# Order of turns, spreads and C copies in the scan steps of a twelve-layer decoder kernel

## The chip, the core and the metric

One Trainium2 chip, one of its cores. The metric is the device time of one launch in microseconds (us). The kernel before took 2616.81, 2618.38 and 2629.36 us in three runs, median 2618.38 us. The profile shown here is of one further execution, which took 2617.74 us.

## The reference

Twelve layers, four decoder blocks of attention, cross block and feed-forward, each followed by a layer norm over 4 sequences of 256 tokens, width 256. The change touches only the cross block of the first two decoder blocks (layers 1 and 4), a selective state-space scan: 256 inner channels, 16 states.

```python
x = einsum('ed,bld->bel', in_proj_w, ctx); u = silu(causal_conv4(x) + conv_b)
x_dbl = einsum('ke,bel->bkl', x_proj_w, u)          # 8 rows dt, 16 rows B, 16 rows C
delta = softplus(dt_proj_w @ dt_lo + dt_proj_b); A = -exp(A_log)
def step(state, t):                                  # for each token t
    state = state * exp(delta_t * A) + (delta_t * u_t) * B_t
    y_t = sum_n state[n] * C_t[n]
y = (y + D * u) * silu(z)                            # z: the layer's own input
```

## The kernel before, in words

The program has a queue of instructions for each engine, written out in layer order; semaphores join them, and every engine executes its queue strictly in order. TensorE (PE), VectorE (DVE), ScalarE (ACT), GpSimd (POOL) and the DMA queue of SyncE (SP) take part. SP issues only the loads of weights for these layers.

The class `StateSpace` makes the scan over time one DVE instruction for each state and half of the tokens. So a layer has 32 steps (`STEPS`): steps 0 to 15 are the 16 states for tokens 0 to 511, steps 16 to 31 the same for tokens 512 to 1023. Channels lie on partitions, in two groups (`CH`), so a step works on 128 x 1024 values. One step k is:

- *spread* (`tensor_spread`, L824, PE): two matmuls with a picking matrix write row B of state k to all partitions of PSUM bank 4, and row C to bank 5. There is one bank for each, so spread k waits until ACT has copied C of step k-1 (`s_c_read`) and until DVE has read B of step k-1 (`s_driven`).
- *drive* (`vector_drive`, L925, DVE): `du` times bank 4, into one of two PSUM buffers (banks 0 and 1, or 2 and 3).
- *exponentials* (L1003, ACT, two instructions) make the decay of step k, in one of two buffers, so they wait for scan k-2.
- *C copy* (L1008, ACT): bank 5 to SBUF, into one of two buffers `c`, so it waits for the product of step k-2 (`s_outed`).
- *scan* (L936, DVE): decay and drive into the state, one of two buffers.
- *product* (L1054, POOL): state times C, into `out`, one of two buffers, so it waits for the turns of step k-2 (`s_added`).
- *turns* (`tensor_add`, L842, PE): eight transposing matmuls add `out` to the sums in PSUM banks 6 and 7. After step 15 and after step 31 eight more add the skip term, and ACT reads the sums out (*y read*, L1016, `scalar_y`). The turns of step 16 wait for the first y read, since they start the sums anew.

The order is set by slots. `vector_slot(s)` puts drive s+1 ahead of scan s. `scalar_slot(s)` puts the work of step s+1 on ACT. `tensor_slot(s)` puts spread s+1 and then the turns of step s-1 on PE. `gpsimd_slot(s)` is product s. Layer norm and the next layer follow, and they need the last y read.

A class `SmallHeads` can host such a scan beside its own work (`hosts`), but `build` makes both scan layers unhosted, so its line in the diff adds nothing to this program.

Of the kernel before, what the change touches and what calls it, by code (L numbers as in the profile page):

```python
# [22 lines left out]
ALU = mybir.AluOpType  # L23
ACT = mybir.ActivationFunctionType
# [8 lines left out]
CH = D // P  # L33
# [4 lines left out]
BANK = 512  # L38
# [32 lines left out]
class Arena:  # L71


    def __init__(self, tensor, words):
        self.tensor, self.words, self.at = tensor, words, 0
# [24 lines left out]
def bcast(ap, axis, n):  # L100

    shape = list(ap.shape)
    return ap.unsqueeze(axis).broadcast_to(shape[:axis] + [n] + shape[axis:])
# [76 lines left out]
class LayerNorm:  # L180
# [43 lines left out]
    def tensor(self, pe):  # L224
        e, nc, l = self.e, self.e.nc, self.l
        for pair in range(TILES // 2):
            pe.wait_ge(e.x_ready, TILES * l + 2 * pair + 2)
            for half in range(2):
                for c in range(CH):
                    last = nc.tensor.transpose(e.bank[self.turn_bank(pair)][:, c * D + half * P:c * D + half * P + P],  # L230
                                               e.x_tok[:, 2 * pair + half, c * P:(c + 1) * P], e.ident[:])
            last.then_inc(e.xt_psum, 1)
# [14 lines left out]
class SmallHeads:  # L247
# [137 lines left out]
    def tensor(self, pe):  # L385
# [121 lines left out]
            if t % 2:  # L507
                last.then_inc(e.y_ready, 1)
        if self.hosts:
            self.beside.tensor_slot(pe, STEPS)  # L510

    def proj_bank(self, blk, s, half):
        return (0 if blk or self.hosts else 4) + 2 * s + half
# [183 lines left out]
STEPS = HALVES * STATES  # L697
# [6 lines left out]
class StateSpace:  # L704
# [10 lines left out]
    def __init__(self, e, l, arena, name, room=None):  # L715
        self.e, self.l, self.name = e, l, name
        self.hosted = room is not None
        a, big = arena, e.big
# [12 lines left out]
        splitting = a.take(2 * TOKENS)  # L731
        self.rest = splitting[:, 0:TOKENS]
        self.mid = splitting[:, TOKENS:TOKENS + BANK].bitcast(BF16)
        self.low = splitting[:, TOKENS + BANK:2 * TOKENS].bitcast(BF16)
        self.c = splitting[:, 0:2 * BANK].rearrange("p (k t) -> p k t", k=2)
        if not self.hosted:
            big.reset()
        self.u = big.take(CH, TOKENS)
# [12 lines left out]
        s = e.sem  # L751
# [97 lines left out]
    def tensor_slot(self, pe, s):  # L849
        if s + 1 < STEPS:  # L850
            self.tensor_spread(pe, s + 1)
        if s:
            self.tensor_add(pe, s - 1)

    def tensor(self, pe):
        if not self.hosted:
            self.wait_start(pe)
            self.tensor_in(pe)
            self.tensor_low(pe)
            self.tensor_dt(pe)  # L860
            self.tensor_spread(pe, 0)
            for s in range(STEPS + 1):
                self.tensor_slot(pe, s)

    def vector_conv(self, dve):
# [126 lines left out]

    def scalar_step(self, act, k):
        a, n = self.e.nc.scalar.activation, k % STATES
        if k == 0:
            act.wait_ge(self.s_cleared, 1)
            act.wait_ge(self.s_delta, 1)
            self.e.act_chain.join(act)
        else:
            act.wait_ge(self.s_scanned, k - 1)  # L1000
        for j in range(CH):
            seqs = lambda ap: ap.rearrange("p (b t) -> p b t", b=2)[:, :, 1:]
            last = a(seqs(self.decay[:, k % 2, j, :]), seqs(self.delta[:, j, self.cols(k)]), ACT.Exp, scale=self.a_neg[:, j, n:n + 1])  # L1003
        last.then_inc(self.s_decay, 1)
        act.wait_ge(self.s_bc_psum, k + 1)
        if k >= 2:
            act.wait_ge(self.s_outed, k - 1)
        a(self.c[:, k % 2, :], self.e.bank[5][:], ACT.Copy).then_inc(self.s_c_read, 1)  # L1008

    def scalar_y(self, act, half):  # L1010
        a = self.e.nc.scalar.activation
# [37 lines left out]
    def gpsimd_slot(self, pool, s):  # L1049
        pool.wait_ge(self.s_c_read, s + 1)  # L1050
        pool.wait_ge(self.s_scanned, s + 1)
        if s >= 2:
            pool.wait_ge(self.s_added, s - 1)
        self.e.nc.gpsimd.tensor_tensor(self.out[:, s % 2], self.state[:, s % 2], bcast(self.c[:, s % 2, :], 1, CH), ALU.mult).then_inc(self.s_outed, 1)  # L1054

    def gpsimd(self, pool):
        if not self.hosted:
# [1359 lines left out]
```

## Time and profile before

| what | value |
|---|---|
| median of three runs | 2618.38 us |
| the profiled execution, its span | 2617.74 us, 2616.0 us |
| PE, its weight loads | 1932.2 us (74%), 1283.9 us (49%) |
| DVE | 1528.2 us (58%) |
| ACT | 832.8 us (32%) |
| POOL | 557.0 us (21%) |
| chain that ended last, share of the span | PE 55%, DVE 30%, ACT 5%, issue 5%, POOL 3% |

The shares are averages over twelve layers with different limits. The scans run from 198.50 to 330.28 us and from 562.81 to 696.15 us of the span; the rest of the program is not touched. In the timeline a row is one instruction, or some of one line in a row (x8). In brackets stands how long the engine was idle before it, and which instruction released it. Rows of PE are matmuls, rows of PEld the weight loads beside them.

### The profile page before, as it was taken

The numbers are of one execution on the slowest core, as the hardware profiler recorded it, in microseconds if no ns is written. First come the engines' busy times: TensorE is split into PE (matmuls) and PEld (weight loads), VectorE is DVE, ScalarE is ACT, GpSimd is POOL, SyncE is SP. The second block draws the span as 40 slices with busy tenths as digits, with TensorE's granted clock in tenths as the row PEclk, the third lists the DMA queues.
The fourth block names the chain that finished last, engine by engine and source line by source line (L and its number), as shares of the span: only waits on it lengthen the run. The fifth ranks groups of instructions, "written<-read, shape, count | busy, mean of one in ns | idle before, by whom it ended". The sixth has DMA issues, their size and how long they took to land.

```text
span 2616.0 us, 28127 instructions
## 1 busy us (share of the span) xinstructions
PE 1932.2 (74%) x9950; PEld 1283.9 (49%) x9950; DVE 1528.2 (58%) x2480; ACT 832.8 (32%) x2085; POOL 557.0 (21%) x353
## 2 busy tenths in 40 slices
PE   5646678646546766888889846445999999999886
PEld 3523444324323455666667524324666765555743
DVE  4368757677795814555553299997466324445114
ACT  1344402254322053555552111111455214444000
POOL 1304410014302042333331055564000000000010
PEclk9975577655567988888889877776999999999966
DMA  3000020100000110000010100000001000000000
GB/s 104 7 33 1 0 55 5 50 1 0 8 33 15 22 42 9 13 11 12 12 56 1 73 0 0 0 0 0 8 10 50 1 15 9 12 12 19 6 27 16
DMA packets 25737, 49.11 MB, mean 19 GB/s; under 512 B 6262, under 2 KB 19603, under 8 KB 24092
## 3 DMA queue, kind: packets, MB, share of 16 engines
q1 hardware_dynamic: 25644, 47.85, 6.1%
q8 instruction: 60, 0.98, 0.2%
q14 instruction: 33, 0.27, 0.0%
HBM read 42.20 MB, written 1.05 MB: 17 GB/s over the span
## 4 chain that ended last, share of the span: by engine, by line
PE 55%; DVE 30%; ACT 5%; issue 5%; POOL 3%; SPq 1%; DMA 1%; DVEq 0%; ACTq 0%; POOLq 0%
PE banks L1309 7%; PE banks L1278 7%; PE banks L1318 7%; PE banks L1247 6%; DVE big L1989 5%; PE banks L1301 4%; DVE big L1985 3%; PE banks L842 3%; DVE big L556 2%; PE banks L1543 2%; DVE big L936 2%; POOL big L1054 2%; PE banks L463 2%; PE banks L474 2%; DVE arena L1365 1%
## 5 line engine op out<-in xcount | busy, mean ns | idle before, releaser
L1384 DVE COPY arena<-banks 128x512 f32<-128x512 f32 x196 | 135.6, 692 | 329.8 <-PE banks L1301 326.6
L222 POOL TENSOR_TENSOR ln_rstd<-ln_var_eps,neg_half 128x2 f32<-128x2 f32 x48 | 37.4, 780 | 1057.8 <-DVE ln_var_eps L210 1057.8
L1278 PE MATMUL banks<-big 128*128 128x256 f32 x784 | 235.6, 413 | 6.0 <-ACT big L1420 4.4
L1309 PE MATMUL banks<-arena,big 128*128 128x256 f32 x784 | 227.5, 414 | 6.3 <-DVE arena L1384 6.3
L1441 ACT ACTIVATE arena<-banks,arena 128x256 f32<-128x256 f32 x392 | 193.4, 500 | 62.2 <-DVE arena L1358 43.1
L842 PE MATMUL banks<-ident,big 128*128 128x128 f32 x544 | 130.4, 419 | 94.0 <-POOL big L1054 90.0
L1459 ACT ACTIVATE big<-banks 128x256 f32 (+1 forms) x196 | 75.3, 384 | 348.1 <-PE banks L1309 348.1
L842 PEld LDWEIGHTS banks<-ident,big 128*128 128x128 f32 x544 | 105.3, 219 | 149.5 <-POOL big L1054 135.3
L1318 PE MATMUL banks<-arena,big 128*128 128x256 f32 x784 | 176.8, 385 | 1.9 <-ACT big L1459 1.9
L1247 PE MATMUL banks<-x_feat,arena 128*128 128x512 f32 x392 | 177.5, 596 | 0.0
L1309 PEld LDWEIGHTS banks<-arena,big 128*128 128x128 f32 x784 | 140.7, 197 | 64.4 <-DVE arena L1384 43.0
L1365 DVE TENSOR_SCALAR arena<-arena 128x256 f32<-128x256 f32 x392 | 166.1, 466 | 6.9
L1352 DVE TENSOR_REDUCE arena<-banks 128x2 f32<-128x512 f32 x196 | 134.2, 685 | 60.5 <-PE banks L1278 42.5
L1318 PEld LDWEIGHTS banks<-arena,big 128*128 128x128 f32 x784 | 148.5, 191 | 29.1 <-issue 6.2
L1054 POOL TENSOR_TENSOR big<-big,arena 128x1024 f32<-128x1024 f32 x64 | 128.4, 2007 | 149.8 <-DVE big L936 104.4
L1278 PEld LDWEIGHTS banks<-big 128*128 128x128 f32 x784 | 136.5, 201 | 33.7 <-ACT big L1420 8.8
L1949 PE MATMUL banks<-ident,big 128*128 128x128 f32 x128 | 29.9, 425 | 162.7 <-POOL big L2038 162.7
L936 DVE TENSOR_TENSOR_SCAN big<-big,banks 128x1024 f32<-128x1024 f32 x64 | 145.7, 2279 | 0.0
L1989 DVE SCALAR_TENSOR_TENSOR big<-big,arena 128x2048 f32<-128x2048 f32 x32 | 141.2, 4411 | 1.1
L1301 PE MATMUL banks<-ident,arena 128*128 128x128 f32 x784 | 128.1, 289 | 18.4 <-DVE arena L1365 18.4
L203 DVE TENSOR_TENSOR x_tok<-x_tok,banks 128x512 f32<-128x512 f32 x40 | 27.4, 685 | 184.2 <-PE banks L1318 100.1
L1301 PEld LDWEIGHTS banks<-ident,arena 128*128 128x128 f32 x784 | 99.4, 148 | 65.6 <-DVE arena L1365 33.0
(311 smaller groups left out, 3514.6 us busy)
## 6 DMA issues: line engine op xcount, KB each, us to landing
big<-big SPq DMA_DIRECT2D x32, 64.0 KB, 2.3
arena<-in_L0f_w SPq DMA_DIRECT2D x1, 2048.0 KB, 8.0
arena<-in_L1a_wo SPq DMA_DIRECT2D x1, 2048.0 KB
arena<-in_L1f_gv SPq DMA_DIRECT2D x1, 2048.0 KB
arena<-in_L2a_qk_w SPq DMA_DIRECT2D x1, 2048.0 KB
big<-big SPq DMA_DIRECT2D x64, 32.0 KB
arena<-in_L2x_wo SPq DMA_DIRECT2D x1, 2048.0 KB
arena<-in_L2x_q_w SPq DMA_DIRECT2D x16, 128.0 KB, 2.0
```

What stands on the lines that cost most here:

```text
L842: ins = e.nc.tensor.matmul(e.bank[6 + t // 2][:, at:at + P], src[:, j, t * P:(t + 1) * P], e.ident[:], is_transpose=True, start=(first and ...
L936: self.e.nc.vector.tensor_tensor_scan(flat(self.state[:, s % 2]), flat(self.decay[:, s % 2]), flat(self.drive[s % 2]), 0.0, ALU.mult, ALU. ...
L1054: self.e.nc.gpsimd.tensor_tensor(self.out[:, s % 2], self.state[:, s % 2], bcast(self.c[:, s % 2, :], 1, CH), ALU.mult).then_inc(self.s_ou ...
L1247: last = mm(B[half][:], self.q_w[:, head_par, c, :], e.x_feat[:, c, cols], start=(c == 0), stop=(c == CH - 1))
L1278: last = mm(ps[:, h * SEQ:(h + 1) * SEQ], q[:, b * SEQ + h * P:b * SEQ + (h + 1) * P], k[:, b * SEQ:(b + 1) * SEQ], start=True, stop=not s ...
L1301: last = nc.tensor.transpose(B[4 + u % 2][:, kc * SEQ + h * P:kc * SEQ + (h + 1) * P], self.probs[:, u % 2, h, kc * P:(kc + 1) * P], e.ide ...
L1309: last = mm(slot, self.v[:, 2 * b + kc, :], self.probs_t[:, u % 2, kc, :], start=(kc == 0), stop=(kc == 1))
L1318: last = mm(e.y_bank(t), self.out[:, h, t * P:(t + 1) * P], wo[h], start=(h == 0), stop=(h == self.heads - 1 and not self.bias))
L1365: last = v.tensor_scalar(self.probs[:, u % 2, h, :], self.probs[:, u % 2, h, :], self.inv[:, u % 2, h:h + 1], None, ALU.mult)
L1384: v.tensor_copy(self.probs_t[:, u % 2].rearrange("p a b -> p (a b)"), B[4 + u % 2][:]).then_inc(self.turn_read, 1)
L1441: last = a(self.probs[:, u % 2, h, :], B[2 + u % 2][:, h * SEQ:(h + 1) * SEQ], ACT.Exp, bias=self.neg_max[:, u % 2, h:h + 1], scale=scale, ...
L1989: v.scalar_tensor_tensor(self.chosen[h], self.sums, self.final[:, h, 7:8], self.sums, ALU.is_ge, ALU.mult, accum_out=self.kept[:, h:h + 1] ...
```

## The change

Three things are moved or made larger; no instruction is added or removed.

- `tensor_slot(s)` puts the turns of step s-2, not s-1, behind spread s+1, and so there is one more slot at the end. The matching line in `SmallHeads` is not used here.
- `c` has four buffers of 512 values in place of two, in the room that the splitting of B and C into bf16 parts used before the steps. The copy of step k waits for product k-4, not k-2.
- In `scalar_step` the C copy, with its waits, stands ahead of the two exponentials of the same step. For step 0 it stands ahead of the waits for the cleared decay buffer and for delta, too.

```diff
--- before.py
+++ after.py
@@ -507,7 +507,7 @@
             if t % 2:
                 last.then_inc(e.y_ready, 1)
         if self.hosts:
-            self.beside.tensor_slot(pe, STEPS)
+            self.beside.tensor_slot(pe, STEPS), self.beside.tensor_slot(pe, STEPS + 1)
 
     def proj_bank(self, blk, s, half):
         return (0 if blk or self.hosts else 4) + 2 * s + half
@@ -732,7 +732,7 @@
         self.rest = splitting[:, 0:TOKENS]
         self.mid = splitting[:, TOKENS:TOKENS + BANK].bitcast(BF16)
         self.low = splitting[:, TOKENS + BANK:2 * TOKENS].bitcast(BF16)
-        self.c = splitting[:, 0:2 * BANK].rearrange("p (k t) -> p k t", k=2)
+        self.c = splitting.rearrange("p (k t) -> p k t", k=4)
         if not self.hosted:
             big.reset()
         self.u = big.take(CH, TOKENS)
@@ -849,8 +849,8 @@
     def tensor_slot(self, pe, s):
         if s + 1 < STEPS:
             self.tensor_spread(pe, s + 1)
-        if s:
-            self.tensor_add(pe, s - 1)
+        if s >= 2:
+            self.tensor_add(pe, s - 2)
 
     def tensor(self, pe):
         if not self.hosted:
@@ -859,7 +859,7 @@
             self.tensor_low(pe)
             self.tensor_dt(pe)
             self.tensor_spread(pe, 0)
-            for s in range(STEPS + 1):
+            for s in range(STEPS + 2):
                 self.tensor_slot(pe, s)
 
     def vector_conv(self, dve):
@@ -992,6 +992,10 @@
 
     def scalar_step(self, act, k):
         a, n = self.e.nc.scalar.activation, k % STATES
+        act.wait_ge(self.s_bc_psum, k + 1)
+        if k >= 4:
+            act.wait_ge(self.s_outed, k - 3)
+        a(self.c[:, k % 4, :], self.e.bank[5][:], ACT.Copy).then_inc(self.s_c_read, 1)
         if k == 0:
             act.wait_ge(self.s_cleared, 1)
             act.wait_ge(self.s_delta, 1)
@@ -1002,10 +1006,6 @@
             seqs = lambda ap: ap.rearrange("p (b t) -> p b t", b=2)[:, :, 1:]
             last = a(seqs(self.decay[:, k % 2, j, :]), seqs(self.delta[:, j, self.cols(k)]), ACT.Exp, scale=self.a_neg[:, j, n:n + 1])
         last.then_inc(self.s_decay, 1)
-        act.wait_ge(self.s_bc_psum, k + 1)
-        if k >= 2:
-            act.wait_ge(self.s_outed, k - 1)
-        a(self.c[:, k % 2, :], self.e.bank[5][:], ACT.Copy).then_inc(self.s_c_read, 1)
 
     def scalar_y(self, act, half):
         a = self.e.nc.scalar.activation
@@ -1051,7 +1051,7 @@
         pool.wait_ge(self.s_scanned, s + 1)
         if s >= 2:
             pool.wait_ge(self.s_added, s - 1)
-        self.e.nc.gpsimd.tensor_tensor(self.out[:, s % 2], self.state[:, s % 2], bcast(self.c[:, s % 2, :], 1, CH), ALU.mult).then_inc(self.s_outed, 1)
+        self.e.nc.gpsimd.tensor_tensor(self.out[:, s % 2], self.state[:, s % 2], bcast(self.c[:, s % 4, :], 1, CH), ALU.mult).then_inc(self.s_outed, 1)
 
     def gpsimd(self, pool):
         if not self.hosted:
```

PE's queue, at the start of a scan layer and in the middle and at the end of it (L824 the spreads, two matmuls for each step; L842 the turns, eight for each step; L230 the transposes of the layer norm that follows):

```order
 L803 MATMUL banks<-big,arena 104x512 x4
 L814 MATMUL banks<-arena 128x512 x4
-L824 MATMUL banks<-arena 128x512 x6
+L824 MATMUL banks<-arena 128x512 x8
 L842 MATMUL banks<-ident,big 128x128 x8
 L824 MATMUL banks<-arena 128x512 x2
```

Four spreads, not three, stand ahead of the first turns. From there on spreads and turns take turns as before, each group of turns one spread later.

```order
 L842 MATMUL banks<-ident,big 128x128 x8
 L824 MATMUL banks<-arena 128x512 x2
-L842 MATMUL banks<-ident,big 128x128 x8
-L824 MATMUL banks<-arena 128x512 x2
-L842 MATMUL banks<-ident,big 128x128 x32
+L842 MATMUL banks<-ident,big 128x128 x40
 L230 MATMUL banks<-ident,x_tok 128x128 x16
```

At the layer's end five groups of eight turns, not four, stand behind the last spread.

ACT's queue at the first steps (before, L1003 are the exponentials and L1008 the C copy; in the changed kernel the copy is L998 and the exponentials are L1007; L991 ends the softplus, L1023 scales `u` for the skip term):

```order
 L985 ACTIVATE big<-big 128x512 x4
 L991 ACTIVATE big<-big,arena 128x2048 x4
-L1003 ACTIVATE big<-big,arena 128x2x255 x2
-L1008 ACTIVATE arena<-banks 128x512
-L1003 ACTIVATE big<-big,arena 128x2x255 x2
-L1008 ACTIVATE arena<-banks 128x512
+L998 ACTIVATE arena<-banks 128x512
+L1007 ACTIVATE big<-big,arena 128x2x255 x2
+L998 ACTIVATE arena<-banks 128x512
+L1007 ACTIVATE big<-big,arena 128x2x255 x2
 L1023 ACTIVATE big<-big,arena 128x512 x4
```

Copy and exponentials of each step have changed places. The queues of DVE, POOL and SP are the same in both kernels.

## Rows read from the trace of the kernel before

**Rows 1.** Groups by line: name, shapes, count; busy us, mean ns; idle before.
```profile
L936 DVE TENSOR_TENSOR_SCAN big<-big,banks 128x1024 f32<-128x1024 f32 x64 | 145.7, 2279 | 0.0
...
L1054 POOL TENSOR_TENSOR big<-big,arena 128x1024 f32<-128x1024 f32 x64 | 128.4, 2007 | 149.8 <-DVE big L936 104.4 <-ACT arena L1008 42.0 <-issue 3.4
...
L1003 ACT ACTIVATE big<-big,arena 128x510 f32<-128x510 f32 x128 | 85.2, 712 | 99.9 <-DVE big L936 84.6 <-POOL big L1047 15.3
...
L925 DVE TENSOR_TENSOR banks<-big,banks 128x1024 f32<-128x1024 f32 x64 | 78.7, 1229 | 55.1 <-PE banks L824 52.2
...
L1008 ACT ACTIVATE arena<-banks 128x512 f32<-128x512 f32 x64 | 38.2, 597 | 51.8 <-POOL big L1054 51.8
```

**Rows 2.** Timeline, steady steps, first scan layer: start, length (us), engine, line, operation [idle].
```profile
232.43 2.28 DVE L936 TENSOR_TENSOR_SCAN big<-big,banks 128x1024 f32<-128x1024 f32 x1
...
234.81 1.23 DVE L925 TENSOR_TENSOR banks<-big,banks 128x1024 f32<-128x1024 f32 x1
234.84 2.00 POOL L1054 TENSOR_TENSOR big<-big,arena 128x1024 f32<-128x1024 f32 x1 [2.94 <-DVE big L936]
235.95 2.28 DVE L936 TENSOR_TENSOR_SCAN big<-big,banks 128x1024 f32<-128x1024 f32 x1
...
236.89 1.97 PE L842 MATMUL banks<-ident,big 128*128 128x128 f32 x8 [2.12 <-POOL big L1054]
236.93 0.60 ACT L1008 ACTIVATE arena<-banks 128x512 f32<-128x512 f32 x1 [0.86 <-POOL big L1054]
...
238.36 2.00 POOL L1054 TENSOR_TENSOR big<-big,arena 128x1024 f32<-128x1024 f32 x1 [1.53 <-ACT arena L1008]
...
238.65 1.06 PE L824 MATMUL banks<-arena 96*128 96x512 bf16 x2
239.75 1.23 DVE L925 TENSOR_TENSOR banks<-big,banks 128x1024 f32<-128x1024 f32 x1 [1.52 <-PE banks L824]
...
240.89 2.28 DVE L936 TENSOR_TENSOR_SCAN big<-big,banks 128x1024 f32<-128x1024 f32 x1
```

**Rows 3.** Timeline, first steps of the first and of the second scan layer.
```profile
194.26 1.23 DVE L925 TENSOR_TENSOR banks<-big,banks 128x1024 f32<-128x1024 f32 x1
...
196.29 1.04 PE L824 MATMUL banks<-arena 96*128 96x512 bf16 x2 [21.25 <-ACT arena L1008]
...
197.37 1.23 DVE L925 TENSOR_TENSOR banks<-big,banks 128x1024 f32<-128x1024 f32 x1 [1.88 <-PE banks L824]
...
198.50 2.28 DVE L936 TENSOR_TENSOR_SCAN big<-big,banks 128x1024 f32<-128x1024 f32 x1
...
562.81 2.28 DVE L936 TENSOR_TENSOR_SCAN big<-big,banks 128x1024 f32<-128x1024 f32 x1
```

**Rows 4.** Timeline, turn from first to second half, first scan layer.
```profile
265.80 3.67 PE L842 MATMUL banks<-ident,big 128*128 128x128 f32 x16 [0.71 <-POOL big L1054]
...
269.27 1.06 PE L824 MATMUL banks<-arena 96*128 96x512 bf16 x2
...
271.26 1.02 ACT L1016 ACTIVATE big<-banks 128x1024 f32<-128x1024 f32 x1
```

**Rows 5.** Timeline, end of the first and of the second scan layer.
```profile
325.82 4.46 DVE L936 TENSOR_TENSOR_SCAN big<-big,banks 128x1024 f32<-128x1024 f32 x2
...
330.19 3.07 DVE L954 TENSOR_TENSOR big<-big,x_feat 128x512 f32<-128x512 f32 x2
...
330.41 2.30 POOL L1054 TENSOR_TENSOR big<-big,arena 128x1024 f32<-128x1024 f32 x1 [0.18 <-DVE big L936]
...
336.98 1.29 DVE L954 TENSOR_TENSOR big<-big,x_feat 128x512 f32<-128x512 f32 x2 [3.71 <-ACT big L1016]
...
691.69 4.46 DVE L936 TENSOR_TENSOR_SCAN big<-big,banks 128x1024 f32<-128x1024 f32 x2
```

**Rows 6.** Windows of L842 alone: stretch, its us, busy (count), clock, DMA.
```profile
236.50:239.00 2.50, 1.97 (x8) 1.57 (x8) 0.50 0.00 0
272.20:273.50 1.30, 1.10 (x8) 0.86 (x8) 1.00 0.00 0
```

## The prediction

> **What bounds the kernel now.** I read the page first, and its 74% for PE says little, because the change touches only the two scan layers. So I read the groups by line for the lines of a scan step, then the timeline of some steps in the middle, and then the two ends of the stage, where a rule for the middle may fail.
>
> In the groups by line [rows 1] the reader should see that DVE does one drive (1.229 us) and one scan (2.279 us) for each step, 3.51 us, and that no other engine has so much: ACT two exponentials and a copy (2 x 0.712 + 0.597 = 2.02 us), POOL one product (2.007 us). Yet DVE idles 55.1 us ahead of its drives, 52.2 of it released by the spreads on PE. That idle time is what can be had here.
>
> The timeline [rows 2] shows its shape. From 234.81 on DVE does drive and scan without a gap: scan 232.43 to scan 235.95 is 3.52 us, the period of a step without a wait. The next drive waits 1.52 us. From scan 232.43 to scan 240.89, two steps, are 8.46 us, or 4.23 for a step. I follow the ring of waits through these rows: the scan ends at 234.71, its product on POOL runs from 234.84 to 236.84, its turns on PE start at 236.89, the spread queued behind them starts at 238.65 and ends at 239.71, the drive starts at 239.75 and the scan at 240.89. Each row starts 0.04 to 0.13 us after the end of the one before, or overlaps it on one engine; nothing in the ring is free. It takes 8.46 us and comes back to DVE two steps on. So a scan step is bound by a ring of DVE, POOL and PE, and its weak place is that a spread, which needs nothing from the product, stands behind turns that do.
>
> **The moved turns.** No instruction is added. With the turns of step s-2 behind spread s+1, the same ring (scan, product, turns, next spread, drive, scan) comes back three steps on: 8.46 / 3 = 2.82 us a step. That is under DVE's 3.52, so the wait goes and DVE is next. I check the other candidates for a period.
>
> PE's own turn: turns and spread back to back run from 236.89 to 239.71 [rows 2], 2.82 us. In the new rhythm I put the end of a drive at 0. The spread runs from 0.13 to 1.19. The product of two steps ago ends 0.90 after this point: its scan ended as this drive started, at -1.23, plus 0.13 and 2.00. So the turns start behind the spread at about 1.2 and end at 3.2, before the next drive ends at 3.52. There are 0.3 us to spare, the smallest margin of this argument.
>
> Buffers: a product takes 2.00 and its turns 1.97 us, which with two `out` buffers is about 2 us a step, and product s waits for turns s-2, ended some 2.7 us before it (3.2 against 5.9). The state buffer returns after product and scan, 4.4 us in two steps. No new wait decides there.
>
> **The four buffers for C and the order on ACT.** With the turns moved alone the next ring would be: scan, product (ends 236.84), C copy of two steps on (236.93 to 237.53 in [rows 2]), spread, drive, scan. With 0.13 for the handoff to PE the spread would run from 237.66 to 238.72, the drive start at 238.76 and the scan at 239.90: 7.47 us in two steps, 3.74 a step. That is 0.22 over DVE's, so both parts are needed for the whole gain. With four buffers the copy waits for a product four steps back, which has long ended. The copy ahead of the exponentials then runs as soon as its spread ends, at 1.2 to 1.9 in my rhythm, in a gap where ACT otherwise waits for the scan that ends at 2.28; the exponentials run from 2.35 to 3.7 and are needed at 7.0. So head-of-line waiting on ACT is covered by 3.3 us. I price it at nothing; were the cover gone, the exponentials would be late by the copy's 0.60 us.
>
> **The start.** Before, drive 0 starts at 194.26 and ends at 195.49, but spread 1 starts only at 196.29, after the copy behind the first exponentials, and drive 1 follows at 197.37 [rows 3]. The first copy is now done before drive 0. Spread 1 starts at 195.62, 0.67 earlier, and so do drive 1 and the first scan. The second layer has the same queues, so 0.67 there too.
>
> **The turn between the halves.** The sixteen turns of step 15 take 3.67 us, the next spread starts 3.47 after their start, and the y read takes 1.02 [rows 4]. I count from the end of scan 15. The product ends at 2.13, spread 18 at about 2.5. The sixteen turns run from 2.5 to 6.2, spread 19 from 6.0 to 7.0. Drive 19 is due at 7.1 (two periods and 0.1). It just fits. The y read runs from about 6.3 to 7.3, the turns of step 16 from 7.35 to 9.3, spread 20 ends at 10.2, drive 20 is due at 10.6. So nothing is added here; if one of these is late by some tenths, each layer loses as much once, under 1 us.
>
> **The end.** The last two scans stand together (4.46 us for both in [rows 5]), and then product 31 and its turns follow as before. The turns of step 30 must still precede those of step 31, and they end before product 31 does in both orders. Nothing won or lost. TensorE has granted clock 0.50, the 1.2 GHz level, for most of this stage, and eight turns take 1.97 us; in a short stretch at 1.00, the 2.4 GHz level, they took 1.10 [rows 6]. If the denser PE gets the higher level, only the 24 turns at the end are on the path, and the products stand between them: at most about 1 us a layer. I count 0 and keep it for the lower end.
>
> **The sum.** First layer: scan 0 starts at 198.50 - 0.67 = 197.83. Thirty periods of 3.52 are 105.6, so scan 30 starts at 303.43 and scan 31 ends at 307.89, against 325.82 + 4.46 = 330.28 before [rows 3, 5]: 22.4 us. Second layer: 562.81 - 0.67 + 105.6 + 4.46 = 672.20, against 696.15: 23.9 us. Together 46.3. As a check, 15 waits of 1.52 less a normal gap of 0.1 are 21 us a layer. The profiled execution took 2617.74 us, so 2571.4; its time is 0.64 below the median, which gives 2572. Everything behind the layers waits for the y read and moves with it. Each 0.1 us by which the period misses 3.52 costs 6.0 us.
>
> **Rivals.**
>
> *PE becomes the bound.* Its two waits in a step now fall apart, the spread behind the drive and the turns behind the spread, so the pipeline may not stay filled. Unoverlapped, a turn of PE is 0.13 + 1.06 + 0.05 + 1.97 = 3.21 us; with a weight load of 0.20 (1.57 / 8 [rows 6]) exposed at each wait 3.61, and with another 0.13 as handoff 3.74. That is 0.09 to 0.22 over DVE, or 5 to 13 us: 2577 to 2585. Against it: in rows 2 the spread starts behind the turns with no such gap. DVE would then still show short waits for L824.
>
> *DVE and POOL share something and slow each other, and it ends slower.* This has its place at the drives, which now always start as a product starts. The row for it is at the layer's end: the two products L954 on DVE, beside a product on POOL, take 3.07 us, and two without it 1.29; the one on POOL takes 2.30, not 2.00 [rows 5]. If each step paid the same 1.78 us, the period would be 5.30 and the kernel would take 2572 + 60 x 1.78 = 2679. From a stretch of 0.77 us a step (46.3 / 60) it is slower than before. Against it: the product at 234.84 covers the whole drive at 234.81 and the start of the scan at 235.95, and both keep their usual 1.23 and 2.28 [rows 2]; half of the steps before were already like this, and the mean of all 64 drives is 1229 ns [rows 1].
> The Trainium skill ("SBUF — State Buffer", section "Who interferes with whom") says that a DVE instruction with two inputs in SBUF contends with a GpSimd instruction that reads SBUF, and one with a single input there, outside certain fast modes, does not. L954 reads `big` and `x_feat`, the drive `big` and PSUM `banks`: by that rule, and the trace agrees, the price is 0 and the time stays 2572.
>
> *The wait only moves.* If the ring were bound on POOL's wait for the copies (1.53 us ahead of the product at 238.36 [rows 2]) or on ACT behind spreads, DVE would wait ahead of its scans instead and the period stay 4.23: 2618. Against it: the ring above closes without that copy, to 0.01 us.
>
> **How the numbers follow.** The forecast has a chance of 0.83, with an own range of 2565 to 2578: 1 us a layer for each end effect, and a period of up to 3.6. PE as the bound 0.11, the wait only moved 0.03, DVE and POOL in each other's way 0.03. The range 2562 to 2588 takes in the higher clock below and PE as the bound above, and leaves out the last two. A measurement of this kernel can tell about 0.5%, 13 us, from no change, so below 2605 is faster: 0.83 + 0.11 = 0.94. Same 0.03, slower 0.03.
>
> **What would show it.** In the profile after: scans every 3.52 us; the idle time ahead of L925 down from 55.1 to under 5 us, nearly all at the starts; drive, scan and product with their old means of 1229, 2279 and 2007 ns; ACT's idle time ahead of the C copy put down to the spreads, no longer to POOL; the last scans ending near 308 and 650 us (672 less the first layer's 22). The prediction is wrong if DVE still waits for L824 in the middle of the layers (PE bound), if its drives grow longer, or if it begins to wait ahead of L936.

## The result, and the profile after

The changed kernel took 2577.66 us (median of 4 runs, 2571.83 to 2591.45), the kernel before 2617.82 (4 runs, 2616.81 to 2629.36). The ratio is 0.984, 95% interval 0.981 to 0.987: faster by 1.6%. The profiled execution took 2571.83 us, its span 2570.1, against 2617.74 and 2616.0 before. Run again beside the experiments it had ratios of 0.9815 (0.978 to 0.985) and 0.9817 (0.977 to 0.986).

The groups by line of the changed kernel (the copy is now L998, the exponentials L1007) answer to [rows 1]:

```profile
L936 DVE TENSOR_TENSOR_SCAN big<-big,banks 128x1024 f32<-128x1024 f32 x64 | 145.7, 2279 | 0.0
...
L1054 POOL TENSOR_TENSOR big<-big,arena 128x1024 f32<-128x1024 f32 x64 | 128.4, 2007 | 103.6 <-DVE big L936 100.5 <-ACT arena L998 3.1
...
L1007 ACT ACTIVATE big<-big,arena 128x510 f32<-128x510 f32 x128 | 85.1, 712 | 40.1 <-DVE big L936 25.7 <-POOL big L1047 14.4
...
L925 DVE TENSOR_TENSOR banks<-big,banks 128x1024 f32<-128x1024 f32 x64 | 78.7, 1229 | 8.9 <-PE banks L824 2.4
...
L998 ACT ACTIVATE arena<-banks 128x512 f32<-128x512 f32 x64 | 38.3, 598 | 62.5 <-PE banks L824 62.5
```

The mean durations of scan, product, exponentials, drive and copy are the old ones to within 1 ns, and DVE has no idle time ahead of its scans. What fell is idle time: 55.1 to 8.9 us ahead of the drives, of which the spreads on PE release 2.4, and no longer 52.2. ACT's copies now wait for spreads and no longer for products.

The timeline of a step in the middle, which answers to [rows 2]:

```profile
226.01 1.23 DVE L925 TENSOR_TENSOR banks<-big,banks 128x1024 f32<-128x1024 f32 x1
226.04 2.00 POOL L1054 TENSOR_TENSOR big<-big,arena 128x1024 f32<-128x1024 f32 x1 [1.53 <-DVE big L936]
227.15 2.28 DVE L936 TENSOR_TENSOR_SCAN big<-big,banks 128x1024 f32<-128x1024 f32 x1
...
227.39 1.01 PE L824 MATMUL banks<-arena 96*128 96x512 bf16 x2 [0.81 <-DVE banks L925]
...
228.19 1.91 PE L842 MATMUL banks<-ident,big 128*128 128x128 f32 x8
228.44 0.60 ACT L998 ACTIVATE arena<-banks 128x512 f32<-128x512 f32 x1 [1.17 <-PE banks L824]
229.46 1.33 ACT L1007 ACTIVATE big<-big,arena 128x510 f32<-128x510 f32 x2 [0.43 <-DVE big L936]
229.53 1.23 DVE L925 TENSOR_TENSOR banks<-big,banks 128x1024 f32<-128x1024 f32 x1
...
230.91 1.01 PE L824 MATMUL banks<-arena 96*128 96x512 bf16 x2 [0.80 <-DVE banks L925]
```

DVE goes from drive to scan to drive: 226.01 to 229.53 is 3.52 us, each step. The spread starts 0.15 us after the drive's end, and behind it stand turns of a product that had ended at 228.04, so PE is never kept from a spread. It idles 0.81 us ahead of each, waiting for the drive. The start answers to [rows 3]:

```profile
202.45 1.23 DVE L925 TENSOR_TENSOR banks<-big,banks 128x1024 f32<-128x1024 f32 x1
...
203.83 1.01 PE L824 MATMUL banks<-arena 96*128 96x512 bf16 x2 [20.61 <-DVE banks L925]
204.88 1.23 DVE L925 TENSOR_TENSOR banks<-big,banks 128x1024 f32<-128x1024 f32 x1 [1.20 <-PE banks L824]
...
206.01 2.28 DVE L936 TENSOR_TENSOR_SCAN big<-big,banks 128x1024 f32<-128x1024 f32 x1
```

Drive 1 starts 2.43 us after drive 0 (3.11 before), scan 0 3.56 after it (4.24 before). At the turn between the halves, which answers to [rows 4], spread 19 starts 3.42 us after the sixteen turns and ends at 267.90, and drive 19 starts on time at 268.29:

```profile
263.42 3.62 PE L842 MATMUL banks<-ident,big 128*128 128x128 f32 x16
...
266.84 1.06 PE L824 MATMUL banks<-arena 96*128 96x512 bf16 x2
268.29 1.23 DVE L925 TENSOR_TENSOR banks<-big,banks 128x1024 f32<-128x1024 f32 x1
```

The ends of the two layers answer to [rows 5]:

```profile
311.70 4.46 DVE L936 TENSOR_TENSOR_SCAN big<-big,banks 128x1024 f32<-128x1024 f32 x2
...
316.07 3.07 DVE L954 TENSOR_TENSOR big<-big,x_feat 128x512 f32<-128x512 f32 x2
...
316.29 2.31 POOL L1054 TENSOR_TENSOR big<-big,arena 128x1024 f32<-128x1024 f32 x1 [0.18 <-DVE big L936]
...
318.65 3.67 PE L842 MATMUL banks<-ident,big 128*128 128x128 f32 x16 [0.52 <-POOL big L1054]
...
649.12 4.46 DVE L936 TENSOR_TENSOR_SCAN big<-big,banks 128x1024 f32<-128x1024 f32 x2
...
656.07 2.58 PE L842 MATMUL banks<-ident,big 128*128 128x128 f32 x16 [0.52 <-POOL big L1054]
```

From the start of scan 0 to the end of scan 31 it is 110.15 us (206.01 to 316.16) and 110.14 us (543.44 to 653.58), in place of 131.78 and 133.34. That is 21.6 and 23.2 us less. The rest of the program is where I had not looked. This table has the time in us from the start of one layer norm's last write of `x_feat` to that of the next, as the rows of L238 in the traces give it; layers 5 to 10 are together:

| layers | before | after | difference | after, third profile | before, again |
|---|---|---|---|---|---|
| 0 | 145.86 | 154.04 | +8.18 | 143.66 | 154.30 |
| 1 (scans) | 204.02 | 182.29 | -21.73 | 181.51 | 204.22 |
| 2 | 85.74 | 84.68 | -1.06 | 85.65 | 85.85 |
| 3 | 74.54 | 69.06 | -5.48 | 74.51 | 74.45 |
| 4 (scans) | 205.27 | 182.59 | -22.68 | 181.35 | 205.38 |
| 5 to 10 | 1766.67 | 1766.47 | -0.20 | 1770.10 | 1770.21 |
| 11 | 132.83 | 129.86 | -2.97 | 132.76 | 129.87 |

The two scan layers give 44.4 of the 45.9 us; layers that were not touched gave 9.7 and took 8.2. The last two columns, of experiments below, show that most of this comes and goes in both kernels. Layer 3's short time does not stand in them; two other kernels below (B in SBUF, and each third drive on POOL) have the same 69.06.

Within layer 4 something went the other way. Its first scan starts 52.8 us after the last write of layer 3's norm has ended, 52.1 before, where 51.4 was to be had; in the two other profiles of the changed kernel it is 51.4. So the first profile has a loss of 1.4 us there, all of it ahead of drive 0.

### The profile page after: what moved, and what is told of

Its sections match the earlier page's. It is cut to its first block, busy times and chain, and to the rows that moved or that the text cites. A ratio compares the mean times of both kernels' runs of the same rounds, so it can differ in the third digit from the quotient of the medians.

```text
span 2570.1 us, 28114 instructions
## 1 busy us (share of the span) xinstructions
PE 1921.5 (75%) x9941; PEld 1275.6 (50%) x9950; DVE 1528.0 (59%) x2480; ACT 832.6 (32%) x2085; POOL 557.0 (22%) x353
## 3 DMA queue, kind: packets, MB, share of 16 engines
HBM read 42.20 MB, written 1.05 MB: 17 GB/s over the span
## 4 chain that ended last, share of the span: by engine, by line
PE 53%; DVE 34%; issue 5%; ACT 4%; SPq 1%; POOL 1%; DMA 1%; DVEq 0%; ACTq 0%; POOLq 0%
PE banks L1309 7%; PE banks L1278 7%; PE banks L1318 7%; PE banks L1247 6%; DVE big L936 6%; DVE big L1989 6%; PE banks L1301 4%; DVE big L1985 3%; DVE big L556 3%; PE banks L1543 2%; PE banks L463 2%; PE banks L474 2%; DVE arena L1365 1%; DVE big L1637 1%; DVE arena L1994 1%
## 5 line engine op out<-in xcount | busy, mean ns | idle before, releaser
L1949 PE MATMUL banks<-ident,big 128*128 128x128 f32 x128 | 30.0, 425 | 162.1 <-POOL big L2038 162.1
L824 PE MATMUL banks<-arena 96*128 96x512 bf16 x128 | 63.2, 595 | 96.7 <-DVE banks L925 95.5
L842 PE MATMUL banks<-ident,big 128*128 128x128 f32 x544 | 124.0, 406 | 7.9 <-POOL big L1054 6.9
```

## The experiments

Scans 0 to 31 of each scan layer, in us, with the time of each kernel. In the two kernels profiled more than once the scans repeat within 0.1 us a layer, while the span varies by up to 9.4. The ratio is to runs of before on the same chip; their median was 2629.10 beside the fourth, 2620.91 beside the others:

| kernel | period | first layer | second | median us | ratio to before |
|---|---|---|---|---|---|
| before | 3.53 and 4.94 by turns | 131.78 | 133.34 | 2620.91 | 1 |
| moved turns alone | 3.52 and 3.85 by turns | 115.06 | 115.36 | 2593.60 | 0.9905 (0.988-0.993) |
| copy ahead, four buffers, alone | 3.52 and 4.94 by turns | 133.45 | 133.54 | 2628.34 | 1.0022 (1.0005-1.0038) |
| moved turns, copy ahead, two buffers | 3.52 and 3.85 by turns | 116.06 | 115.78 | 2600.57 | 0.9894 (0.984-0.994) |
| moved turns, four buffers | 3.52 | 110.09 | 110.19 | 2579.37 | 0.9828 (0.979-0.986) |
| the full change, again | 3.52 | 110.09 | 110.11 | 2575.56 | 0.9815 (0.978-0.985) |

**Moved turns alone.** The turns move as in the change, with one slot more at the end; the excerpt has the turns.

```diff
-        if s:
-            self.tensor_add(pe, s - 1)
+        if s >= 2:
+            self.tensor_add(pe, s - 2)
```

> Only the turns move behind the next spread; C keeps two buffers and its place behind the exponentials. My theory (rings of waits): the ring through the C copy (scan 2.28, product 2.00, copy 0.60, spread 1.06, drive 1.14, handoffs) takes 7.47 us in two steps, so the period of a step falls from 4.23 to 3.74 us, scans 0 to 31 take 30 x 3.74 + 4.46 = 116.7 us in each layer (131.8 and 133.3 before), and the kernel about 32 us less than before, near 2586; ahead of its drives DVE still waits some 0.2 us a step, released by spreads that wait for the C copy. Rival 1 (the moved turns are all that matters): period 3.52, 110.1 us a layer, about 45 us less. Rival 2 (the wait was the copy's, not the turns'): period 4.23, no gain.

Measured 115.06 and 115.36 us a layer, 34.7 us less in the scans than before, and 27 us less in the time of the kernel (2593.60 against 2620.91), which misses the expected 2586. In its profile layer 6, which nothing here touches, took 231.0 us, and 218.8 to 221.7 in the profiles of before and of the full change; why is not known. Two other kernels below had 231.0 there too. Timeline of this kernel, where L1008 is the C copy and L1003 the exponentials:

```profile
220.86 2.00 POOL L1054 TENSOR_TENSOR big<-big,arena 128x1024 f32<-128x1024 f32 x1 [1.84 <-DVE big L936]
...
222.95 0.60 ACT L1008 ACTIVATE arena<-banks 128x512 f32<-128x512 f32 x1 [0.86 <-POOL big L1054]
...
223.61 1.03 PE L824 MATMUL banks<-arena 96*128 96x512 bf16 x2 [1.10 <-ACT arena L1008]
...
224.68 1.23 DVE L925 TENSOR_TENSOR banks<-big,banks 128x1024 f32<-128x1024 f32 x1 [0.42 <-PE banks L824]
225.82 2.28 DVE L936 TENSOR_TENSOR_SCAN big<-big,banks 128x1024 f32<-128x1024 f32 x1
```

The ring is the one expected: product, copy, spread, drive. It closes in 7.37 us for two steps, not 7.47, since the spread follows the copy by 0.06 us, not 0.13. So the moved turns alone bring three quarters of the gain in the scans (34.7 of 44.8 us), and then the C copy binds.

**Copy ahead and four buffers, turns unmoved.** An excerpt; `c` has four buffers, and the copy's old place behind the exponentials is gone, as in the change.

```diff
+        act.wait_ge(self.s_bc_psum, k + 1)
+        if k >= 4:
+            act.wait_ge(self.s_outed, k - 3)
+        a(self.c[:, k % 4, :], self.e.bank[5][:], ACT.Copy).then_inc(self.s_c_read, 1)
         if k == 0:
```

> Only ACT's side of the change: four buffers for C and the copy ahead of the exponentials; the turns stay where they were. My theory: the ring through product, turns and the spread behind them is untouched, period 4.23 us, scans 0 to 31 131 to 133 us a layer; the earlier first copy saves 0.67 us a layer, so about 1 us less than before, not to be told from no change. ACT's waits for the product go, POOL's waits for the copies too, and nothing comes of it. Rival 2 (the wait was the copy's): period 3.5 to 3.7, 30 to 45 us less.

Measured 133.45 and 133.54 us a layer and 2628.34 us, 0.2% over before. Groups by line of this kernel:

```profile
L925 DVE TENSOR_TENSOR banks<-big,banks 128x1024 f32<-128x1024 f32 x64 | 78.7, 1229 | 55.6 <-PE banks L824 52.5
...
L998 ACT ACTIVATE arena<-banks 128x512 f32<-128x512 f32 x64 | 38.2, 597 | 143.6 <-PE banks L824 143.6
```

DVE's wait for spreads is 52.5 us, as before, though the copy no longer waits for products at all. So the rival that the copy held DVE falls. That its first layer takes 1.7 us more than before is not the rhythm; at the turn of the halves two steps take 4.75 and 5.64 us (5.23 and 3.55 before). I did not expect it. The rows put most of it down to the clock: the turns of step 16 and the spread behind them took 1.97 and 1.06 us, where before they had met the higher level and took 1.10 and 0.61. The y read, which now stood right behind the exponentials, came 0.35 us later after the start of the sixteen turns.

**Moved turns and four buffers, copy left behind the exponentials.** The turns move as in the change; the excerpt has the copy.

```diff
-        if k >= 2:
-            act.wait_ge(self.s_outed, k - 1)
-        a(self.c[:, k % 2, :], self.e.bank[5][:], ACT.Copy).then_inc(self.s_c_read, 1)
+        if k >= 4:
+            act.wait_ge(self.s_outed, k - 3)
+        a(self.c[:, k % 4, :], self.e.bank[5][:], ACT.Copy).then_inc(self.s_c_read, 1)
```

> The moved turns and four buffers for C, with the copy left behind the exponentials. My theory: the copy of step k starts 1.33 us after scan k-2 ends, ends at about 2.05, its spread at 3.2, and the next drive is due at 3.6, so the period is 3.52 us all the same, 110.1 us a layer; only the first step loses its 0.67 us a layer. About 44 us less than before, within 2 us of the full change. Rival (the order on ACT is needed): the spread is late behind the copy, DVE waits 0.1 to 0.3 us a step, period 3.6 to 3.8, 6 to 17 us slower than the full change.

110.09 and 110.19 us a layer: the whole rhythm. Its groups by line:

```profile
L925 DVE TENSOR_TENSOR banks<-big,banks 128x1024 f32<-128x1024 f32 x64 | 78.7, 1229 | 10.3 <-PE banks L824 3.9
...
L824 PE MATMUL banks<-arena 96*128 96x512 bf16 x128 | 63.8, 600 | 100.1 <-ACT arena L1008 96.2 <-DVE banks L925 2.8 <-DVE arena L898 1.1
```

PE's idle time is now put down to the copy (96.2 us), not to the drive, so the copy does come later; but DVE waits for spreads only 3.9 us in all, 1.5 more than with the full change. From drive 0 to scan 0 it is 4.24 us again, and 3.56 with the full change. So the order on ACT is worth its 0.67 us at the start of a layer, and beyond it at most 0.1 us a layer.

**Moved turns, copy ahead, two buffers.** The C copy stands ahead as in the full change, with `k % 2` and the wait for `s_outed` at k - 1.

> Moved turns, and the copy ahead of the exponentials, but with the old two buffers for C. My theory: the copy still waits for the product two steps back, so the ring through the copy decides as with the turns alone (3.52 and 3.85 us by turns there, scans 115.1 to 115.4 us a layer); the order on ACT changes nothing but the start, so 115 us a layer again. Rival (head-of-line blocking on ACT): the copy at the head now keeps the exponentials back until the product is done, the decay becomes late, DVE waits ahead of its scans and the period exceeds 3.69 us by some tenths, up to 0.60, the copy's length: 118 to 133 us a layer.

116.06 and 115.78 us, 1.0 and 0.4 more than with the turns alone. Its groups by line:

```profile
L936 DVE TENSOR_TENSOR_SCAN big<-big,banks 128x1024 f32<-128x1024 f32 x64 | 145.9, 2279 | 0.9 <-ACT big L1007 0.9
...
L925 DVE TENSOR_TENSOR banks<-big,banks 128x1024 f32<-128x1024 f32 x64 | 78.7, 1229 | 19.4 <-PE banks L824 15.9
```

Head-of-line blocking (an instruction that waits at the head of a queue keeps back those behind it) is there, but small: DVE waits 0.9 us in all ahead of scans for late exponentials, 0.60 of it ahead of the last scan of the first layer. The rival's 0.60 us a step came in that one step and not in the rhythm.

**More work on PE.** The first matmul of each spread done twice (`(0, 0, 1)`), and both done twice (shown, the second line cut off at its end):

```diff
-        for n in range(2):
+        for n in (0, 0, 1, 1):
             last = self.e.nc.tensor.matmul(self.e.bank[4 + n][:], ...
```

> The full change, with the first matmul of each spread done twice (same result): 0.53 us more for PE in each step. PE idles 0.81 us ahead of each spread in the profile of the full change. My theory: it still fits, period 3.52, scans 110.1 to 110.3 us a layer, PE's idle time per step down to about 0.3. Rival (PE nearly the bound, as in my forecast's first rival): the 0.3 us of margin that I gave are overdrawn by 0.2, period 3.7, 116 us a layer.

> The full change, with both matmuls of each spread done twice: 1.06 us more for PE in each step, more than the 0.81 us that it idles. My theory: now PE binds. Counting from the end of a spread: drive starts at 0.04 and ends at 1.27; the turns begin 0.2 us before 0, and the next spread 1.76 after their start, at 1.56, ending at 3.63; the next drive 3.67. Period 3.67, scans near 114.6 us a layer, about 9 us more than the full change, with DVE idle 0.15 us ahead of each drive. Rival (waits between PE's groups empty its pipeline, 0.2 us each): period 3.9 or more, 121 us a layer. Rival (PE doesn't matter at all): 110.1.

Both took 110.1 us a layer (110.08 and 110.08, 110.09 and 110.08), and 2580.46 and 2583.86 us. The first came as expected. The second broke my expectation: at the 1.2 GHz level its 1.06 us of added work are more than the 0.81 us that PE had idle, and there was no loss. Windows 220 to 240 us, of the kernels with one and with two more, and of the full change; the clock is the number behind the last "(x...)":

```profile
220.00:240.00 20.00, 12.64 (x64) 8.01 (x65) 19.48 (x12) 11.10 (x18) 11.63 (x6) 0.83 0.01 1
```

```profile
220.00:240.00 20.00, 10.53 (x66) 6.92 (x67) 19.48 (x12) 10.90 (x17) 11.98 (x6) 1.00 0.01 2
```

```profile
220.00:240.00 20.00, 15.64 (x58) 10.23 (x59) 19.48 (x12) 10.48 (x17) 10.98 (x6) 0.50 0.00 1
```

With more work PE was granted the 2.4 GHz level, for part of this window and for all of it, where the full change stayed at the 1.2 GHz level. Over the scans of each layer the mean granted clock was 0.87 and 0.95, against 0.53. So PE's longer turn took less time.

In some steps the kernel with one more matmul stood at the 1.2 GHz level, and there it shows PE's margin:

```profile
231.55 1.44 PE L824 MATMUL banks<-arena 96*128 96x512 bf16 x3 [0.84 <-DVE banks L925]
232.79 1.91 PE L842 MATMUL banks<-ident,big 128*128 128x128 f32 x8
235.07 0.94 PE L824 MATMUL banks<-arena 96*128 96x512 bf16 x3 [0.38 <-DVE banks L925]
```

The three matmuls take 1.44 us in place of 1.01, the turns the usual 1.91, and 0.38 us of idle time are left of 0.81, in the same period of 3.52. The timeline of the kernel with both matmuls twice:

```profile
224.88 1.02 PE L824 MATMUL banks<-arena 96*128 96x512 bf16 x4 [1.62 <-DVE banks L925]
...
225.74 1.04 PE L842 MATMUL banks<-ident,big 128*128 128x128 f32 x8
...
227.03 1.23 DVE L925 TENSOR_TENSOR banks<-big,banks 128x1024 f32<-128x1024 f32 x1
```

Four matmuls take 1.02 us, where two took 1.01, and the turns 1.04 in place of 1.91; from the spread's start to the end of the turns it is 1.90 us in place of 2.71. So this kernel did not try PE's margin at the 1.2 GHz level; the rows above did. It shows instead that the stage has none of its time from PE: with the turns at nearly half their length, DVE's rhythm is 3.52 all the same.

**B read from SBUF by the drive.** ACT copies both banks at once (an excerpt, with `...` where a line is shortened):

```diff
-        a(self.c[:, k % 4, :], self.e.bank[5][:], ACT.Copy).then_inc(self.s_c_read, 1)
+        a(self.bc[:, k % 4], self.e.banks[:, 4:6, :], ACT.Copy).then_inc(self.s_c_read, 1)
-        ... self.drive[k % 2], self.du[:, :, self.cols(k)], bcast(self.e.bank[4][:], 1, CH), ALU.mult)
+        ... self.drive[k % 2], self.du[:, :, self.cols(k)], bcast(self.bc[:, k % 4, 0, :], 1, CH), ALU.mult)
```

> The full change, but ACT copies the spread of B with that of C (1024 in place of 512 values, 1.02 us by the y read of the same size), and the drive on DVE reads B from SBUF, so it has two inputs there and runs beside the product on POOL. It measures the disputed cost of DVE and POOL in each other's way. By the rule (two SBUF inputs contend, one doesn't) and the start of the drive 0.03 us ahead of the product: the product waits for the drive, its row grows from 2.00 to about 3.2 us, and the period stays at 3.52 to 3.6. If the product gets in first, the drive grows from 1.23 to up to 3.2 us and the period to 5.5 (170 us a layer). If nothing contends: both keep 1.23 and 2.00 and the period is 3.52. In no case does that say that the changed kernel pays anything: its drive has one SBUF input.

2592.41 us, 114.02 and 114.03 us a layer, at a period of 3.52 to 3.53 but for two steps of 5.42, where the copy stood on ACT behind the skip scaling or the y read and the drive was 1.0 and 1.8 us late for that reason. The timeline shows both orders of arrival:

```profile
209.72 2.00 POOL L1054 TENSOR_TENSOR big<-big,arena 128x1024 f32<-128x1024 f32 x1 [6.92 <-DVE big L936]
...
210.73 2.08 DVE L925 TENSOR_TENSOR banks<-big,arena 128x1024 f32<-128x1024 f32 x1 [1.15 <-ACT arena L998]
...
225.68 1.23 DVE L925 TENSOR_TENSOR banks<-big,arena 128x1024 f32<-128x1024 f32 x1
225.71 3.05 POOL L1054 TENSOR_TENSOR big<-big,arena 128x1024 f32<-128x1024 f32 x1 [0.47 <-ACT arena L998]
```

Where the product was first (209.72), the drive took 2.08 us, ending 1.09 us after the product. Where the drive was first by 0.03 us (225.68), it kept its 1.23 and the product took 3.05 us, 1.05 more; that is so in most steps (55 of the 64 products took 3.04 to 3.06 us; their mean is 2.93). By the section of the Trainium skill named in the prediction ("SBUF — State Buffer", "Who interferes with whom") a VectorE instruction with two inputs in SBUF contends with a GpSimd instruction that reads SBUF, and the issue order decides who blocks. The trace agrees: the later one was slowed, and by nearly the time that it stood beside the other (0.85 of 0.99 us, 1.05 of 1.20). In the changed kernel, whose drive has one input in PSUM, the products have their 2.007 us.

**The full change, and the kernel before, profiled again.**

> The full change unaltered, on the same chip as the three parts. Scans 0 to 31 take 110.1 us in each layer, 21.7 and 23.2 us less than before. The time in between: in its first profile layer 0, which is not touched, took 8.2 us longer than in the profile of before, at a lower granted clock between 80 and 120 us of the span. My theory: this is how the clock happens to rise in that layer, and has nothing to do with the change, so it comes and goes between executions of one kernel; the time is then 2570 to 2592 us and the spans of the two scan stages do not vary. Rival: the change itself costs time in layer 0 or in other layers, and the same 8 us stand there each time.

> The full change once more, for the two kernels beside it. Scans 0 to 31 110.1 us a layer, 2567 to 2592 us. It also gives one more execution of layer 0, which no kernel here touches: it ended at 145.9 us of the span in the profile of before and at 154.0, 151.0 in the two of the full change, 154 in two kernels with moved turns and 143.7 in others. My theory: two or three outcomes of when the clock rises, met by any of the kernels. Rival: the full change fixes the late one.

> The kernel before, unaltered, profiled again: is its layer 0 always the fast one? My theory: it can end near 146 or near 154 us, with the time 8 us apart, and scans 0 to 31 take 131.8 and 133.3 us within 2. Rival: always near 146.

The stages of the scans repeat to 0.1 us: 110.09 and 110.11, 110.13 and 110.11, and for before 131.76 and 133.35. Layer 0 ended at 151.01 and 143.66 us of the span in the full change, at 154.30 in the kernel before. So the late layer 0 is not a trait of the change. The windows 80 to 100 us, within layer 0, of the third profile of the full change and the second of the kernel before:

```profile
80.00:100.00 20.00, 13.05 (x266) 10.35 (x270) 2.55 (x6) 10.48 (x14) 8.60 (x14) 0.88 0.07 16
```

```profile
80.00:100.00 20.00, 13.36 (x176) 10.23 (x176) 1.27 (x3) 6.93 (x10) 5.18 (x9) 0.53 0.06 16
```

In the same stretch of the same work PE had a mean clock of 0.88 in one and 0.53 in the other, and got through 266 matmuls against 176. Nor does it go by kernel: of the thirteen executions profiled after the first, six ended layer 0 near 154, two near 151 and five near 143.7, and the full change was met in all three groups.

**Drives on POOL.** With DVE the bound and POOL idle 1.5 us of each 3.52, a version beyond the change gives POOL some of the drives. POOL writes its drive to SBUF. To keep the scan from two inputs in SBUF, whose price for a scan no run here shows, decay and drive change their places in such a step. State and `out` have four buffers. Excerpts from the edit:

```diff
+        if self.on_pool(k):                       # k % 3 == 2, or k % 4 == 2
+            a(self.b, self.e.bank[4][:], ACT.Copy)
...
+        pair = (self.drive[s % 2], self.pool_drive) if self.on_pool(s) else (self.decay[:, s % 2], self.drive[s % 2])
...
+            self.e.nc.gpsimd.tensor_tensor(self.pool_drive, self.du[:, :, self.cols(k)], bcast(self.b, 1, CH), ALU.mult)
...
-            self.tensor_add(pe, s - 2)
+            self.tensor_add(pe, s - 3)
```

> A version beyond the change: with DVE the bound at 3.52 us a step and POOL idle 1.5 of it, each fourth drive (steps 2, 6, ..., 30) is made by POOL. ACT copies B of such a step to SBUF as well, POOL writes the drive to SBUF, and the decay of that step goes to the PSUM buffer that the drive leaves free, so that the scan still has one SBUF input. State and out get four buffers, and the turns stand three steps behind. My theory: each such step takes DVE 1.24 us less (3.52 - 2.28), 8 in a layer, so scans 0 to 31 take 110.1 - 9.9 = 100.2 us a layer and the kernel about 20 us less than the full change, near 2556. POOL then does 2.05 + 2.00 / 4 us a step, ACT 2.02 + 0.25. Rival 1 (POOL comes late with its drive or holds back the turns): DVE waits ahead of those scans, 0.65 us each if the product goes first, gain 10 us. Rival 2 (DVE and POOL in each other's way after all, the product beside a scan that reads the drive from SBUF): scans grow beside products, no gain or a loss.

> The same with each third drive on POOL (steps 2, 5, ..., 29), 10 in a layer. My theory: scans 0 to 31 take 110.1 - 12.4 = 97.7 us a layer, about 25 us less than the full change, near 2551; POOL does 2.05 + 0.68 = 2.73 us a step of 3.11. Rival (POOL's queue gets late, its drives behind products that it must catch up with): DVE waits ahead of the scans of these steps, and it is no faster than each fourth.

Each fourth drive: 100.03 and 100.39 us a layer, 2559.95 us, ratio to before 0.976 (0.972 to 0.980). Each third: 97.73 and 97.35, 2553.35 us, ratio 0.975 (0.970 to 0.981), while the full change beside them took 2573.61. Both beat the changed kernel, by 14 and 20 us, and the scans came within 0.4 us of what was expected. The groups by line of the second (L951 the scan in its two forms, L1085 the product, L1080 the drive on POOL):

```profile
L1085 POOL TENSOR_TENSOR big<-big,arena 128x1024 f32<-128x1024 f32 x64 | 127.0, 2006 | 4.4 <-DVE big L951 3.7 <-issue 0.4
...
L951 DVE TENSOR_TENSOR_SCAN big<-big,banks 128x1024 f32<-128x1024 f32 x44 | 98.1, 2270 | 0.0
...
L951 DVE TENSOR_TENSOR_SCAN big<-banks,arena 128x1024 f32<-128x1024 f32 x20 | 45.7, 2283 | 0.0
...
L1080 POOL TENSOR_TENSOR arena<-big,arena 128x1024 f32<-128x1024 f32 x20 | 40.0, 1998 | 36.3 <-ACT arena L1017 35.4 <-PE banks L852 1.0
```

Scans and products are not slowed (2.270 and 2.283, 2.006 us), and POOL waits for scans only 3.7 us in all. Three steps take 9.22 us in the rhythm, of which POOL works 8.0 (three products and a drive); ahead of its drives it waits 1 to 1.6 us for ACT's copies. DVE waits ahead of its drives 8.4 us in both layers, the normal gaps and the starts, and never ahead of its scans, so it is still the bound. Against the third profile of the full change the two scan layers won 11.6 and 10.5 us, the scans 12.4 and 12.8: the ends of the layers, with POOL behind, took 0.8 and 0.9 us more, and the first scan of layer 4 started 1.4 us later, as in the first profile of the change. In both of those profiles layer 3 had taken 69.06 us.

## Why the prediction was right, point by point

**The bound and the ring.** Right. The ring of scan, product, turns, the spread behind them and the drive set the 8.46 us for two steps: moving the turns alone breaks it (115.1 us a layer), and clearing everything but the turns leaves it (133.5).

**Two parts for the whole gain.** Right, with one size off: the ring through the copy is 7.37 us for two steps, not 7.47, because the handoff from copy to spread is 0.06 us, not 0.13, and a spread on idle PE 1.03. Four buffers bring 5 us a layer on top of the moved turns.

**The copy ahead of the exponentials.** Priced at nothing in the rhythm, and 0.67 us at the start; measured nothing, and 0.68 (3.56 against 4.24 from drive 0 to scan 0).

**PE's turn.** The conclusion holds, the margin was mis-sized. I laid spread and turns end to end (0.13 + 1.06 + 1.97) and got 0.3 us to spare. In the profile after, the turns start 0.80 after the spread's start and end 2.71 after it, and PE idles 0.81. The first rival put 0.20 us more at each wait; its direction was wrong, since the overlap that I saw in one order of the two groups is there in the other too. With one more matmul, in a step at the 1.2 GHz level, 0.38 us were still left.

**The turn between the halves.** "It just fits" held: 0.39 us to spare.

**The ends.** "Nothing won or lost" was wrong by tenths, through the clock: the last sixteen turns took 3.67 us in the first layer and 2.58 in the second, before 3.11 and 2.80. That is 0.56 lost and 0.22 won.

**DVE and POOL.** Given 0.03; the durations did not move. The experiment with B in SBUF shows that the price exists for a drive with two inputs in SBUF; with `banks` as one of its inputs it does not arise. Even with both inputs in SBUF it would cost DVE only where the product comes first, 0.85 us in the case shown.

**The sum.** Forecast 46.3 us, 2572. The profiled execution gave 45.9, and that it comes so near is in part luck. The scans gave 21.6 and 23.2 as forecast, and the starts won 0.67 us each from drive 0 to scan 0, together 46.2. But layer 4 lost 1.4 ahead of its drive 0 and the first end 0.56, and the second end won 0.22, so the two scan layers gave 44.4; the layers that were not touched gave the other 1.5, as the balance of 9.7 and 8.2. Between the third profile of the change and the second of before the two scan layers gave 22.7 and 24.0, together 46.7. The median of the first four runs is 5.7 us over the forecast, that of all twelve executions of the changed kernel 2575.0. What I had no term for is what untouched layers do from one execution to the next: 8 us in layer 0, where the clock is shown, 5.5 in layer 3, 3 in layer 11.

**The signs.** One was set wrongly: I asked for under 5 us of idle time ahead of L925 and it is 8.9, because the normal gap of 0.1 us ahead of each of 60 drives, hidden within waits before, now counts as idle (about 6 us). And the last scans end at 316 and 654 us, not 308 and 650: the first through layer 0, which was 8.2 us late, the second late by less, since layers 2 and 3 gave 6.5 back.

## What to carry to other kernels

Follow a wait through all the engines until it comes back to the first, and divide the ring's length by the steps that it spans. A spare buffer or a later slot lengthens the span, not the work; the new period is the longest of the rings that are left, the busiest engine among them, so work out the second ring before believing the first (here 3.69 stood between 4.23 and 3.52). When one engine is the bound, look for work of it that an idle one can take. And where a VectorE `tensor_tensor` runs beside GpSimd work, leave one of its inputs in PSUM, as the drive here does. Before you believe a difference of some us between two profiles, compare them stage by stage: here untouched layers moved by more than some of the experiments did.

## What the runs showed of the hardware

- More work raised PE's clock: with spreads of two, three and four matmuls the window 220 to 240 us had 0.50, 0.83 and 1.00, the scans of both layers 0.53, 0.87 and 0.95, and the stage took the same time. At 0.50 PE had idled 0.81 us of each 3.52, with four and at 1.00 1.62. The kernels with drives on POOL, whose PE does the same work in less time, had 0.67 (each fourth) and 0.71 to 0.76 (each third).
- The time at which the clock rises in layer 0 differs between executions of one kernel. The last write of its norm started at 143.7 to 154.0 us in the three profiles of the changed kernel, at 143.7 to 154.4 in all. Against the spread of 24 us between the runs of the changed kernel that is less than half. What decides it no run here shows.
- A drive of two SBUF inputs and a product on GpSimd ran nearly one after the other: 3.05 in place of 2.00 us for the product that came 0.03 us later, 2.08 in place of 1.23 for the drive that came 1.01 us later. A scan with decay in PSUM and drive in SBUF took 2.283 us beside products, and a scan the other way round 2.270.
